# A cross-attention block on one core: steps taken in pairs, and the keys' jobs cut into halves and quarters

## The chip, the cores and the metric

The kernel runs on one core of a Trainium2 chip. The metric is the device time of one execution in microseconds (us). The five engines are named as in the profile: PE is TensorE (PEld its weight loads), DVE is VectorE, ACT is ScalarE, POOL is GpSimd and SP is SyncE, which issues most of the DMAs.

## What is computed

Three layers on x (4 batches x 256 tokens x 256 channels), each with a layernorm ahead and a residual: cross attention to a context of 4096 x 192 for each batch (16 heads of 16), windowed self attention, and a feed-forward with 16 banks of which each token takes two. The change is in the first layer:

```
q = layernorm(x) @ wq.T + bq          # 256 queries per batch
k = ctx @ wk.T + bk                   # 4096 keys per batch
v = ctx @ wv.T + bv
attn = softmax(q k.T / 4)             # per head, 256 x 4096
x = x + (attn v) @ wo.T + bo
```

## The kernel before

**Steps.** Four heads of a batch are a group; there are 16 groups. A group's 4096 keys are 32 tiles of 128, and one tile of a group is a step: 512 steps, numbered n. PE's program is written out by hand in the order of the steps (the loop at L886). A step of the main phase issues three things:

- `scores(n)` (L619, matmuls of L629): four matmuls, keys of tile n against 256 queries, into one of two pairs of PSUM banks. ACT takes the exponential from there into `wts` (L1162, one instruction of 128x1024).
- `max_pair(n + 36)` (L580, matmuls of L599): two matmuls of 512 columns for a group that comes later; DVE reduces each to its row maxima (`reduce_max`, L1412). These maxima are needed before a group's scores begin, hence the lead of 36 steps. From step 36 on the results rotate through three banks (`M_BANKS`), and the pair of number m waits until the first reduction of pair m-1 is done: `e.wait_ge(dve_max, maxed(2 * m - 2))` (L595).
- `weigh(n - 2)` (L634, matmuls of L647): the weights of step n-2 against the values, four heads side by side in four column strips of the array. In two steps of each group (t = 2 and 3) none and two of them are issued.

**Side jobs.** Between steps PE does jobs that `side_jobs(n)` (L133) puts at fixed steps: `("k", f)` projects 1024 keys (L513, 12 matmuls), `("v", b, j)` 256 values (L532), `neg`, `sum`, `norm` and `out` carry a group's maxima and its result. `n + LEAD + K_LEAD` is n + 52, so `("k", f)` stands behind step 16f - 52, and its keys are first read by `max_pair(16f)`, in step 16f - 36: 16 steps later. All jobs and scores share the two bank pairs in turn (`S_NO`), and `bank_pair(job)` (L493) lets PE start a job when ACT has emptied the job two before it.

**The way of a key job.** ACT copies it to `key_f` with the bias (L1169). POOL splits it into a high and a low part (`split_keys`, L1880: a cast, L1883, and a subtraction, L1885). SP copies both parts with twelve DMAs of 128 KB into `keys` (`scatter_k`, L2073; the DMAs are L2071). `max_pair(16f)` waits for all twelve: `e.wait_ge(ld_k[f % 4], k_landed(f))` (L588).

**Values.** In batches 1 to 3 a value job stands at every third step, 16 in a batch, over the first half of its preparation (steps 7, 10, 13, ... counted from where its window begins).

## Time and profile before

| | |
|---|---|
| timed runs (3) | 1278.29, 1279.77 (median), 1281.58 us |
| profiled execution, span from first to last instruction | 1276.3 us |
| median of the timed runs less that span | 3.5 us |
| PE busy | 1239.8 us, 97% of the span |
| DVE busy | 867.8 us, 68% |
| ACT busy | 718.2 us, 56% |
| POOL busy | 258.4 us, 20% |
| step 0 begins / the last scores begin | 74.6 / 917 us |

A matmul in fp32 is recorded as two matmuls of the profile (the weighings are four instructions and eight records). A busy PE is not PE at its peak: the end of a record is modelled, and records overlap. The steps are most of the kernel: some 842 us of the 1276.

### The profile page before, as it was taken

To read this page: it belongs to the slowest core of one execution; us is meant where nothing else is said; L and a number is where in the kernel's file an instruction comes from. 1 tells how busy PE (TensorE), PEld (TensorE's weight loads), DVE (VectorE), ACT (ScalarE), POOL (GpSimd) and SP (SyncE) were. 2 spreads that over 40 slices of the span, in tenths; PEclk is the share of its full clock that TensorE was granted. 3 is DMA by queue.
4 is the path that set the end of the run, shared out by engine and by line. 5 is a ranking of instruction groups with operands and counts; after the bars stand their busy time and mean duration, and the time that the engine had idled before them with its cause. 6 is when DMAs were issued, how large, how long until landed. Compare 5 with 4: busy or idle time off the path is not lost.

```text
span 1276.3 us, 29874 instructions
## 1 busy us (share of the span) xinstructions
PE 1239.8 (97%) x12312; PEld 710.2 (56%) x12312; DVE 867.8 (68%) x1663; ACT 718.2 (56%) x942; POOL 258.4 (20%) x258
## 2 busy tenths in 40 slices
PE   8999999999999999999999999999999998999998
PEld 5454444555544455544445554444466567777787
DVE  4988888766787967588886768894354686223234
ACT  4557777666677867676776767778433320112120
POOL 3322112211111211111211111202011243122210
PEclk9999999999999999999999999999999998999999
DMA  7833573533465554344663433321020005999993
GB/s 223 134 51 59 87 167 53 75 59 59 57 102 124 79 73 61 52 57 100 123 88 53 57 51 57 65 36 52 11 72 2 2 17 222 413 407 401 388 406 117
DMA packets 49847, 150.44 MB, mean 118 GB/s; under 512 B 16944, under 2 KB 23088, under 8 KB 41776
## 3 DMA queue, kind: packets, MB, share of 16 engines
q1 hardware_dynamic: 45552, 136.92, 45.4%
q0 software_dynamic: 2432, 7.11, 1.7%
q10 hardware_dynamic: 1728, 4.49, 1.0%
q8 instruction: 98, 1.61, 0.6%
q14 instruction: 37, 0.30, 0.1%
HBM read 90.03 MB, written 7.08 MB: 76 GB/s over the span
## 4 chain that ended last, share of the span: by engine, by line
PE 88%; DVE 5%; ACT 4%; issue 2%; POOL 1%; DMA 1%; ACTq 0%; DVEq 0%; POOLq 0%
PE psum L647 21%; PE psum L629 15%; PE psum L599 11%; PE psum L513 7%; PE psum L532 6%; PE psum L1072 5%; PE psum L1100 5%; ACT wts L1162 2%; PE psum L1097 2%; PE psum L1066 2%; PE psum L725 2%; DVE part_max L1402 1%; PE psum L845 1%; PE psum L719 1%; PE psum L675 1%
## 5 line engine op out<-in xcount | busy, mean ns | idle before, releaser
L1412 DVE TENSOR_REDUCE part_max<-psum 128x1 f32<-128x512 f32 x952 | 609.7, 685 | 164.0 <-PE psum L599 162.3
L1162 ACT ACTIVATE wts<-psum 128x1024 f32<-128x1024 f32 x512 | 515.8, 1023 | 93.8 <-PE psum L629 92.7
L647 PE MATMUL psum<-wts,vals 128*17 128x256 f32 x4096 | 317.3, 385 | 0.0
L629 PE MATMUL psum<-queries,keys 51*128 51x256 f32 x2048 | 260.6, 333 | 8.2 <-ACT wts L1162 7.0
L629 PEld LDWEIGHTS psum<-queries,keys 51*128 51x128 f32 x2048 | 157.5, 185 | 199.6 <-issue 141.6
L599 PE MATMUL psum<-keys,queries 51*128 51x512 f32 x1024 | 226.5, 438 | 8.7 <-ACT wts L1162 6.0
L647 PEld LDWEIGHTS psum<-wts,vals 128*17 128x17 f32 x4096 | 69.5, 95 | 120.4 <-issue 96.3
L1883 POOL CAST key_high<-key_low 128x1024 fp32r<-128x1024 f32 x31 | 32.2, 1038 | 394.4 <-ACT key_low L1169 390.1
L599 PEld LDWEIGHTS psum<-keys,queries 51*128 51x128 f32 x1024 | 96.7, 184 | 27.4 <-DVE part_max L1402 10.7
L532 PE MATMUL psum<-wv,ctx_in 64*128 64x256 f32 x768 | 100.1, 390 | 3.2 <-ACT key_low L1169 1.8
L1332 ACT ACTIVATE hid<-psum,b1s 128x128 f32<-128x128 f32 (+1 forms) x124 | 31.7, 351 | 113.5 <-PE psum L1072 77.1
L513 PE MATMUL psum<-ctx_in,wk 64*64 64x512 f32 x768 | 93.5, 599 | 0.0
L532 PEld LDWEIGHTS psum<-wv,ctx_in 64*128 64x128 f32 x768 | 70.0, 186 | 32.3 <-issue 17.6
L1169 ACT ACTIVATE key_low<-psum,bk 128x1024 f32<-128x1024 f32 x31 | 34.5, 1114 | 79.4 <-PE psum L513 79.4
L1175 ACT ACTIVATE vals<-psum 128x512 f32<-128x512 f32 x64 | 38.2, 598 | 67.2 <-PE psum L532 67.2
L1885 POOL TENSOR_TENSOR key_low<-key_low,key_high 128x1024 fp32r<-128x1024 f32 x31 | 73.7, 2377 | 2.6
L1921 POOL TENSOR_TENSOR o_norm<-o_raw,inverse 128x256 f32<-128x256 f32 x15 | 11.0, 736 | 268.7 <-ACT inverse L1196 268.7
L1072 PE MATMUL psum<-xTt,w1s 128*128 128x128 f32 x544 | 63.5, 275 | 0.0
L1072 PEld LDWEIGHTS psum<-xTt,w1s 128*128 128x128 f32 x544 | 62.2, 192 | 0.1
L1100 PE MATMUL psum<-w2s,hid 128*128 128x256 f32 x272 | 62.1, 382 | 0.0
L1812 DVE TENSOR_SCALAR hid<-psum,b1s 128x128 f32<-128x128 f32 (+1 forms) x124 | 30.5, 313 | 45.0 <-PE psum L1072 41.9
L1100 PEld LDWEIGHTS psum<-w2s,hid 128*128 128x128 f32 x272 | 50.4, 190 | 11.9 <-issue 5.7
(260 smaller groups left out, 1035.7 us busy)
## 6 DMA issues: line engine op xcount, KB each, us to landing
keys<-key_high SPq DMA_DIRECT2D x256, 128.0 KB, 4.3
w1s<-in_W SPq DMA_DIRECT2D x31, 1024.0 KB
w2s<-in_W SPq DMA_DIRECT2D x31, 1024.0 KB
keys<-key_low SPq DMA_DIRECT2D x128, 128.0 KB, 6.1
ctx_in<-in_ctxT SPq DMA_DIRECT2D x12, 768.0 KB, 8.5
ctx_in<-in_ctxT ACTq DMA_DIRECT2D x4, 768.0 KB, 12.4
rows_y<-in_zeros SPq DMA_DIRECT2D x1, 2048.0 KB, 8.6
queries<-query_high SPq DMA_DIRECT2D x60, 32.0 KB, 5.0
```

Of the source, the lines that this page charges most:

```text
L513: t = e.matmul(bank(S_BANKS[S_NO["k", f] % 2] + odd)[64 * i:64 * i + 64], wk[rows, g % NG, r * 64:(r + 1) * 64], ctx_in[rows, c // 2 + i, ...
L532: m = e.matmul(bank(first + odd)[:, 0:EMB], ctx_in[rows, p, at:at + P], wv[rows, r], start=(r == 0), stop=(r == CB - 1))
L599: e.matmul(bank(LEAD_BANKS[m % 2] + i if m < LEAD else M_BANKS[(2 * m + i) % 3]), queries[g % 3][64 * i:64 * i + STK, hh, qt * P:(qt + 1) ...
L629: m = e.matmul(bank(S_BANKS[S_NO["s", n] % 2] + i)[:, hh * SEQ:(hh + 1) * SEQ], keys[64 * i:64 * i + STK, hh, c, at:at + P], queries[g % 3 ...
L647: i = e.matmul(bank(O_BANK)[32 * j:32 * j + VW, 0:SEQ], vals[:, t, h * VW:(h + 1) * VW], wts[n % NW][:, j * SEQ:(j + 1) * SEQ], start=(t = ...
L1072: i = e.matmul(dst[:, q * P:(q + 1) * P], w1s[w[0]][:, k, hc * P:(hc + 1) * P], xTt[j % 2][:, k], start=(k == 0), stop=(k == KE - 1))
L1100: i = e.matmul(dst, hid[j % 2][:, hc], w2s[w[0]][:, hc], start=(hc == 0), stop=(hc == HC - 1))
L1162: i = e.activation(wts[n % NW], s_bank(job, 2), ACT.Exp, scale=QSCALE)
L1169: i = e.activation(key_f.rearrange("p c k -> p (c k)"), s_bank(job, 2), ACT.Identity, bias=bk[:, hg:hg + 1])
L1175: i = e.activation(vals[:, t:last + 1:CH // P].rearrange("p t (h w) -> p t h w", w=VW)[:, :, :, 0:HD], s_bank(job, 2).rearrange("p (t h w) ...
L1412: e.reduce_max(part_max[g % 2][:, hq, c:c + 1], bank(M_BANKS[n % 3]), AX_X).then_inc(dve_max, 1)
L1885: e.tensor_tensor(key_low, key_f, key_high.bitcast(F32), ALU.subtract).then_inc(split_low, 1)
```

## The change

**Steps in pairs.** PE's order for two steps n and n+1 (n even) is now: scores n, max pair n+36, scores n+1, weigh n-2, weigh n-1, max pair n+37, and then the side jobs of both steps. ACT takes both exponentials and then the side jobs. The lead phase (steps -36 to -1) is as before.

**Key jobs in parts.** `key_parts(f)` gives 1 part for f < 4, 2 parts for f >= 8 with f % 8 in (2, 3, 4), and 4 parts for all others. Parts stand behind steps 16f-52, 16f-50 (halves), and also 16f-48 and 16f-46 (quarters). POOL's split and SP's twelve DMAs come after the last part. K_LEAD, and with it the step in which the keys are first read, are not touched.

**Values.** The 16 value jobs of a batch stand at even steps 6, 8, 10, 16 to 26, 32 to 42 and 48 of the window.

```diff
@@ -130,17 +130,31 @@
         return self.sem
 
 
+def key_parts(f):
+
+    if f < 4:
+        return 1
+    return 2 if f >= 2 * NG and f % (2 * NG) in (2, 3, 4) else 4
+
+
+def key_jobs(f):
+
+    return [("k", f)] if key_parts(f) == 1 else [("k", f, q) for q in range(key_parts(f))]
+
+
+VALUES_AT = (6, 8, 10, 16, 18, 20, 22, 24, 26, 32, 34, 36, 38, 40, 42, 48)
+
+
 def side_jobs(n):
 
     jobs = []
     f, at = divmod(n + LEAD + K_LEAD, 4 * CH // P)
-    if at == 0 and 4 <= f < QUADS:
-        jobs.append(("k", f))
+    if 4 <= f < QUADS and at % 2 == 0 and at // 2 < key_parts(f):
+        jobs.append(key_jobs(f)[at // 2])
     jobs += FIRST_AT.get(n, [])
     b, at = divmod(n + KT, NG * KT)
-    j, off = divmod(at - 7, 3)
-    if 0 < b < BATCH and off == 0 and 0 <= j < KT // 2:
-        jobs.append(("v", b, j))
+    if 0 < b < BATCH and at in VALUES_AT:
+        jobs.append(("v", b, VALUES_AT.index(at)))
     g, at = divmod(n + KT, KT)
     if at == KT - 3 and 0 <= g < GROUPS:
         jobs.append(("neg", g))
```

```diff
@@ -157,24 +171,16 @@
 
 
 S_JOBS = [("k", 0)] + [("v", 0, _j) for _j in range(FIRST_V)] + [("k", 1)]
-for _n in range(-LEAD, STEPS):
-    S_JOBS += ([("s", _n)] if _n >= 0 else []) + side_jobs(_n)
+for _n in range(-LEAD, 0):
+    S_JOBS += side_jobs(_n)
+for _n in range(0, STEPS, 2):
+    S_JOBS += [("s", _n), ("s", _n + 1)] + side_jobs(_n) + side_jobs(_n + 1)
 S_NO = {job: n for n, job in enumerate(S_JOBS)}
 
 
 def maxed(n):
 
     return n // 2 + 1 if n < 2 * LEAD else n + 1 - LEAD
-
-
-def weighed_at(n):
-
-    t = n % KT
-    if n < 3 or (n < STEPS and t == 2):
-        return []
-    if n < STEPS and t == 3:
-        return [n - 3, n - 2]
-    return [n - 2]
 
 
 def v_tiles(j):
```

```diff
@@ -495,13 +501,16 @@
                 if S_NO[job] > 1:
                     e.wait_ge(act_s, S_NO[job] - 1)
 
-            def keys_of(f, part=None, pieces=range(CB)):
-
+            def keys_of(f, part=None, pieces=range(CB), job=None):
+
+                job = job or ("k", f)
                 g, c = f // 2, f % 2 * 4
+                width = CH // key_parts(f)
+                first = job[2] * width if len(job) > 2 else 0
                 pairs = range(2) if part is None else (part,)
                 if 0 in pieces:
                     if part is None:
-                        bank_pair(("k", f))
+                        bank_pair(job)
                     if f == 2:
                         e.wait_ge(ld_wk_rest, 16)
                     for i in pairs:
```

```diff
@@ -510,8 +519,9 @@
                     for i in pairs:
                         for odd in range(2):
                             rows = slice(64 * odd, 64 * odd + 64)
-                            t = e.matmul(bank(S_BANKS[S_NO["k", f] % 2] + odd)[64 * i:64 * i + 64],
-                                         wk[rows, g % NG, r * 64:(r + 1) * 64], ctx_in[rows, c // 2 + i, r * CH:(r + 1) * CH],
+                            at = r * CH + first
+                            t = e.matmul(bank(S_BANKS[S_NO[job] % 2] + odd)[64 * i:64 * i + 64, 0:width],
+                                         wk[rows, g % NG, r * 64:(r + 1) * 64], ctx_in[rows, c // 2 + i, at:at + width],
                                          start=(r == 0), stop=(r == CB - 1))
                 if CB - 1 in pieces:
                     t.then_inc(pe_first if part == 0 else pe_s, 1)
```

```diff
@@ -883,24 +893,33 @@
                 values_of(0, j)
             keys_of(1)
             done_early = 0
-            for n in range(-LEAD, STEPS + 2):
-                jobs = side_jobs(n) if n < STEPS else []
-                if 0 <= n < STEPS:
-                    scores(n)
+            for n in range(-LEAD, 0):
+                max_pair(n + LEAD)
+                for job, piece in LEAD_PIECES.get(n, ()):
+                    lead_piece(job, piece)
+                for job in side_jobs(n):
+                    if job not in LEAD_JOBS:
+                        side_job(job)
+            for n in range(0, STEPS, 2):
+                scores(n)
                 if n + LEAD < STEPS:
                     max_pair(n + LEAD)
-                for m in weighed_at(n):
-                    weigh(m)
-                for job, piece in LEAD_PIECES.get(n, ()):
-                    lead_piece(job, piece)
-                for job in jobs:
-                    if job not in LEAD_JOBS:
+                scores(n + 1)
+                if n:
+                    weigh(n - 2)
+                    weigh(n - 1)
+                if n + LEAD < STEPS:
+                    max_pair(n + 1 + LEAD)
+                for m in (n, n + 1):
+                    for job in side_jobs(m):
                         side_job(job)
-                if n >= LAST * KT + EARLY_FROM and n % 3 != 0 and done_early < 10:
-                    early(done_early)
-                    done_early += 1
-                if n in FIRST_MAX2:
-                    max2(0, FIRST_MAX2.index(n))
+                    if m >= LAST * KT + EARLY_FROM and m % 3 != 0 and done_early < 10:
+                        early(done_early)
+                        done_early += 1
+                    if m in FIRST_MAX2:
+                        max2(0, FIRST_MAX2.index(m))
+            weigh(STEPS - 2)
+            weigh(STEPS - 1)
             e.wait_ge(act_ocopy, GROUPS)
             e.matmul(bank(X_BANK)[:, 0:SEQ], lsel, o_raw, start=True, stop=True).then_inc(pe_lastnorm, 1)
```

```diff
@@ -1166,7 +1185,11 @@
                     if f == 1:
                         e.wait_ge(ld_first, 16 * 6)
                     e.wait_ge(ld_k[(f - 1) % 4], k_landed(f - 1))
-                    i = e.activation(key_f.rearrange("p c k -> p (c k)"), s_bank(job, 2), ACT.Identity, bias=bk[:, hg:hg + 1])
+                    width = CH // key_parts(f)
+                    first = job[2] * width if len(job) > 2 else 0
+                    i = e.activation(key_f[:, :, first:first + width],
+                                     s_bank(job, 2).rearrange("p (c k) -> p c k", c=2)[:, :, 0:width], ACT.Identity,
+                                     bias=bk[:, hg:hg + 1])
                 elif kind == "v":
                     b, j = job[1:]
                     t, last = v_tiles(j)
```

```diff
@@ -1234,15 +1257,18 @@
             for i in range(BT, TT):
                 e.activation(xn1[:, i], x[:, i], ACT.Identity, scale=rstd[:, i:i + 1], bias=sq[:, i:i + 1]).then_inc(act_rows1, 1)
             empty(("k", 1))
-            for n in range(-LEAD, STEPS):
-                if n >= 0:
-                    empty(("s", n))
-                if n > KT and n % KT == 1:
-                    ocopy(n // KT - 1)
+            for n in range(-LEAD, 0):
                 for job in side_jobs(n):
                     empty(job)
                 if n in ONES_AT:
                     key_ones(ONES_AT[n])
+            for n in range(0, STEPS, 2):
+                empty(("s", n))
+                empty(("s", n + 1))
+                if n and n % KT == 0:
+                    ocopy(n // KT - 1)
+                for job in side_jobs(n) + side_jobs(n + 1):
+                    empty(job)
             ocopy(LAST)
```

In POOL's and SP's programs and in the semaphore counts, `("k", f)` became the last part:

```diff
@@ -1878,7 +1904,7 @@
             own = Tally(pool_seq)
 
             def split_keys(f):
-                e.wait_ge(act_s, done(("k", f)))
+                e.wait_ge(act_s, done(key_jobs(f)[-1]))
                 e.wait_ge(ld_k[(f - 1) % 4], k_landed(f - 1))
                 e.tensor_copy(key_high, key_f).then_inc(split_high, 1)
                 e.wait_ge(split_high, f + 1)
```

```diff
@@ -2081,7 +2108,7 @@
                         scatter_pair(f, c, part, ld_k[f % 4])
 
             def load_ctx(b, p):
-                e.wait_ge(pe_s, done(("k", (NG * b - 1) * 2 + p // 2)))
+                e.wait_ge(pe_s, done(key_jobs((NG * b - 1) * 2 + p // 2)[-1]))
                 e.dma_start(ctx_in[:, p], a["ctxT"][b, p]).then_inc(ld_ctx[p], 16)
```

```diff
@@ -2104,7 +2131,7 @@
                     for dst, src in ((lsel, "lsel"), (wo, "woT"), (bv, "bv"), (bo_bc, "bo")):
                         e.dma_start(dst, a[src]).then_inc(ld_w, 16)
                 for job in side_jobs(n - 2):
-                    if job[0] == "k":
+                    if job[0] == "k" and job == key_jobs(job[1])[-1]:
                         scatter_k(job[1])
                         b, at = divmod(job[1], NG * 2)
                         if at >= (NG - 1) * 2 and b + 1 < BATCH:
```

**PE's order in plain steps.** PE, some steps in front of a key job; L629 are scores, L599 a max pair, L647 a weighing. The buffer of `wts` rises by one with each step. Before:

```order
L629 MATMUL psum<-queries_70,keys 128x256 x4
L599 MATMUL psum<-keys,queries_71 128x512 x2
L647 MATMUL psum<-wts_66,vals 17x256 x4
L629 MATMUL psum<-queries_70,keys 128x256 x4
L599 MATMUL psum<-keys,queries_71 128x512 x2
L647 MATMUL psum<-wts_67,vals 17x256 x4
```

And now (L639 scores, L609 max pair, L657 weighing):

```order
L639 MATMUL psum<-queries_70,keys 128x256 x4
L609 MATMUL psum<-keys,queries_71 128x512 x2
L639 MATMUL psum<-queries_70,keys 128x256 x4
L657 MATMUL psum<-wts_66,vals 17x256 x4
L657 MATMUL psum<-wts_67,vals 17x256 x4
L609 MATMUL psum<-keys,queries_71 128x512 x2
```

The two weighings stand together, and between the first and the second max pair there are now one scores and two weighings, between the second and the next first one scores alone.

**PE around a key job.** Before, the whole job (L513) stands behind one step:

```order
L647 MATMUL psum<-wts_68,vals 17x256 x4
L513 MATMUL psum<-ctx_in,wk 64x512 x12
L629 MATMUL psum<-queries_70,keys 128x256 x4
L599 MATMUL psum<-keys,queries_72 128x512 x2
L647 MATMUL psum<-wts_69,vals 17x256 x4
```

Now quarters (L523) stand behind the second max pair of pairs of steps; these are the last two of four, the second of them the part after which the split can begin:

```order
L609 MATMUL psum<-keys,queries_72 128x512 x2
L523 MATMUL psum<-ctx_in,wk 64x128 x12
L639 MATMUL psum<-queries_71,keys 128x256 x4
L609 MATMUL psum<-keys,queries_72 128x512 x2
L639 MATMUL psum<-queries_71,keys 128x256 x4
L657 MATMUL psum<-wts_66,vals 17x256 x4
L657 MATMUL psum<-wts_67,vals 17x256 x4
L609 MATMUL psum<-keys,queries_72 128x512 x2
L523 MATMUL psum<-ctx_in,wk 64x128 x12
```

From the last quarter to the max pair that reads these keys there are four pairs of steps and one scores, where 15 whole steps and one scores stood before.

**ACT.** Parts of a key job are emptied by copies of 128x2x128 (L1190) between two exponentials and the next two:

```order
L1190 ACTIVATE key_low<-psum,bk 128x2x128
L1181 ACTIVATE wts_68<-psum 128x1024
L1181 ACTIVATE wts_69<-psum 128x1024
L1190 ACTIVATE key_low<-psum,bk 128x2x128
L1181 ACTIVATE wts_66<-psum 128x1024
L1181 ACTIVATE wts_67<-psum 128x1024
```

Before, one exponential stood between jobs' copies wherever a step did.

## Rows read from the trace of the kernel before

**Rows 1.** The page: engines' shares of the span, and groups of instructions.

```profile
PE 1239.8 (97%) x12312; PEld 710.2 (56%) x12312; DVE 867.8 (68%) x1663; ACT 718.2 (56%) x942; POOL 258.4 (20%) x258
...
PE 88%; DVE 5%; ACT 4%; issue 2%; POOL 1%; DMA 1%; ACTq 0%; DVEq 0%; POOLq 0%
...
L1412 DVE TENSOR_REDUCE part_max<-psum 128x1 f32<-128x512 f32 x952 | 609.7, 685 | 164.0 <-PE psum L599 162.3
```

**Rows 2.** Timeline of PE, plain steps (start us, us, engine, line, operation).

```profile
403.02 0.50 PE L629 MATMUL psum<-queries,keys 51*128 51x256 f32 x4
403.36 0.45 PE L599 MATMUL psum<-keys,queries 51*128 51x512 f32 x2
403.74 0.63 PE L647 MATMUL psum<-wts,vals 128*17 128x256 f32 x8
404.29 0.50 PE L629 MATMUL psum<-queries,keys 51*128 51x256 f32 x4
```

**Rows 3.** Timeline of DVE over the same steps.

```profile
401.90 4.51 DVE L1412 TENSOR_REDUCE part_max<-psum 128x1 f32<-128x512 f32 x7
```

**Rows 4.** Timeline of PE, the two steps of a group with weighings together.

```profile
395.76 0.50 PE L629 MATMUL psum<-queries,keys 51*128 51x256 f32 x4
396.11 0.45 PE L599 MATMUL psum<-keys,queries 51*128 51x512 f32 x2
396.40 0.40 PE L629 MATMUL psum<-queries,keys 51*128 51x256 f32 x4
397.34 0.50 PE L599 MATMUL psum<-keys,queries 51*128 51x512 f32 x2 [0.55 <-ACT wts L1162]
397.77 1.06 PE L647 MATMUL psum<-wts,vals 128*17 128x256 f32 x16
398.76 0.50 PE L629 MATMUL psum<-queries,keys 51*128 51x256 f32 x4
```

**Rows 5.** Timeline of PE around a key job.

```profile
411.16 2.81 PE L513 MATMUL psum<-ctx_in,wk 64*64 64x512 f32 x24
413.90 0.50 PE L629 MATMUL psum<-queries,keys 51*128 51x256 f32 x4
414.24 0.39 PE L599 MATMUL psum<-keys,queries 51*128 51x512 f32 x2
414.56 0.63 PE L647 MATMUL psum<-wts,vals 128*17 128x256 f32 x8
```

**Rows 6.** Timelines of ACT, POOL and SP: the way of that job.

```profile
414.03 1.11 ACT L1169 ACTIVATE key_low<-psum,bk 128x1024 f32<-128x1024 f32 x1 [2.68 <-PE psum L513]
...
415.21 1.04 POOL L1883 CAST key_high<-key_low 128x1024 fp32r<-128x1024 f32 x1 [4.19 <-ACT key_low L1169]
...
421.39 2.50 SPq L2071 DMA_DIRECT2D keys<-key_low  x4
```

**Rows 7.** DMA issues in 423:424, the last two of its twelve copies.

```profile
keys<-key_low SPq DMA_DIRECT2D x2, 128.0 KB, 6.8
```

**Rows 8.** Timeline of PE: max pairs number 16f, f = 15 to 21.

```profile
410.17 0.50 PE L599 MATMUL psum<-keys,queries 51*128 51x512 f32 x2
...
433.43 0.49 PE L599 MATMUL psum<-keys,queries 51*128 51x512 f32 x2
...
461.88 0.50 PE L599 MATMUL psum<-keys,queries 51*128 51x512 f32 x2
...
491.40 0.50 PE L599 MATMUL psum<-keys,queries 51*128 51x512 f32 x2
...
523.25 0.40 PE L599 MATMUL psum<-keys,queries 51*128 51x512 f32 x2
...
553.73 0.50 PE L599 MATMUL psum<-keys,queries 51*128 51x512 f32 x2
...
579.12 0.50 PE L599 MATMUL psum<-keys,queries 51*128 51x512 f32 x2
```

**Rows 9.** Timelines of PE and ACT around a value job.

```profile
471.99 1.57 PE L532 MATMUL psum<-wv,ctx_in 64*128 64x256 f32 x12
473.20 0.59 PE L629 MATMUL psum<-queries,keys 51*128 51x256 f32 x4
473.63 0.40 PE L599 MATMUL psum<-keys,queries 51*128 51x512 f32 x2
...
473.60 0.60 ACT L1175 ACTIVATE vals<-psum 128x512 f32<-128x512 f32 x1 [1.33 <-PE psum L532]
```

**Rows 10.** Copies by ACT of other sizes, steps 0 to 511.

```profile
L1196 ACT ACTIVATE inverse<-psum 128x256 f32<-128x256 f32 x15 | 5.8, 385 | 3.1 <-PE psum L666 3.1
```

**Rows 11.** Windows in the last layer: us, busy times, granted clock, DMA.

```profile
1055.00:1065.00 10.00, 7.35 (x112) 6.58 (x109) 8.31 (x57) 1.08 (x4) 1.69 (x5) 1.00 0.13 49
1065.00:1068.50 3.50, 3.50 (x25) 2.00 (x26) 3.29 (x12) 0.00 (x0) 0.51 (x1) 0.51 0.35 56
```

More of the change, by code:

```diff
@@ L2106, in _ @@
                 for job in side_jobs(n - 2):
-                    if job[0] == "k":
+                    if job[0] == "k" and job == key_jobs(job[1])[-1]:
                         scatter_k(job[1])
```

5 lines of the change are left out of this document (3 added, 2 removed).

## Prediction

> **What bounds the kernel now.** The page comes first: PE is busy for 97% of the span and 88% of the chain that ended last is PE's, while DVE's reductions take 609.7 us and sat idle for 164 us before them, nearly all of it for PE's max pairs [rows 1]. That reads as PE bound, with DVE held up by PE's long side jobs. But a shares table is a mean over places with different limits, so PE's timeline comes next. A plain step takes 404.29 - 403.02 = 1.27 us (1.28 in most): 0.34 from scores to max pair, 0.38 from there to the weighing, 0.55 to 0.56 to the next scores [rows 2]. Over the same steps DVE ran seven reductions in 4.51 us without a gap, 0.64 each and 1.28 for two [rows 3]. Behind a key job, when DVE had caught up, the max pair's slot is 414.56 - 414.24 = 0.32 instead of 0.38 [rows 5]. So PE alone would need 0.34 + 0.32 + 0.56 = 1.22 us, and it waits some 0.06 in each plain step. What it waits for is the rule that a max pair follows the first reduction of the pair before it. This is a loop, matmul, first reduction, next matmul, and its length can be read where nothing else stands between two max pairs: 397.34 - 396.11 = 1.23 us [rows 4]; in plain steps it closes at 1.28. **PE's own work and the loop over the three banks are near each other, and the loop is what ends last in a plain step.**
>
> **Pairs of steps.** Two weighings in a row take 398.76 - 397.77 = 0.99 instead of 2 x 0.56, and a scores behind a max pair is not preceded by a change of the array's shape. Adding slots for PE alone: scores 0.34, max pair 0.22 (its 0.32 before a weighing less the 0.10 which a change seems to cost; half of what the weighings save is 0.07, so 0.07 to 0.10), scores 0.33, weighings 0.99, second max pair 0.33; the scores that follow then start loaded, 0.23 for 0.34. That is 2.10 us for two steps against 2.44 before. The Trainium skill (TensorEngine Tiling (Array Packing), Key Properties) says that changing the tiling mode drains the engine, where another tile of the same mode does not. The 0.99 agrees with it; by that rule alone every pair would gain 0.3 us, which is the first rival.
>
> The order of the max pairs speaks against it. From the first to the second there now lie a scores and two weighings: 0.29 + 0.33 + 0.99 = 1.61 us. From the second to the next first there is only one scores, so that distance is the loop's, 1.23 to 1.28. A pair of steps without a job thus takes 1.61 + 1.28 = 2.9 us, not 2.1 and not 2 x 1.28 = 2.56. The trace has the same instructions in nearly this order: the two steps where a group's weighings already stand together take 398.76 - 395.76 = 3.00 us, and their second max pair starts late [rows 4]. I take 2.9. In PE's 0.8 us of waiting a job can hide.
>
> **Parts of key jobs.** A whole job takes 413.90 - 411.16 = 2.74 us [rows 5]. Its columns are three rounds of twice 0.43, 2.56 in all, and 0.18 around them; these 0.18 are paid by each part. A quarter is 0.64 + 0.18 = 0.82 (bounds: 0.69, a quarter of the whole, and 1.21, a value job of as many matmuls [rows 9]); a half 1.46. ACT's copy of a quarter takes 0.39 to 0.60, between its copies of 256 and of 512 columns [rows 9, 10]; the second scores of the next pair now needs that copy's bank (the job two before it), and stands only 0.56 behind the first: 0.1 of waiting for a quarter, 0.3 to 0.4 for a half. Pair with a quarter: 0.34 + 0.22 + 0.33 + 0.99 + 0.43 (second max pair, loaded late and with a change of shape, as at 397.34 [rows 4]) + 0.82 + 0.1 = 3.25. With a half: 4.15.
>
> **When the keys land.** This is the largest term. For the job that ended at 413.9, ACT's copy ended at 415.1, POOL's cast at 416.25, SP issued twelve copies until 423.9 [rows 6], and the last two took 6.8 us to land [rows 7]: landed near 430, 16 us after the job's end. The max pair that reads them came at 433.43 [rows 8], so 3.4 us were to spare out of 19.5. Now the split starts behind the last quarter, six steps later, while the reader stays in its step. Less 0.7 for the shorter copy of ACT, the way is 15.4 us. Between them lie four pairs without a key job and one scores, 4 x 2.9 + 0.3 = 11.9 us. **PE waits about 3.5 us at each max pair 16f of a quartered job, with scores, weighings and both other engines queued behind it.** `sum` and `norm` hide in that time. Halves end two steps late and have value jobs behind them: six pairs, no wait.
>
> The stretch from one max pair 16f to the next is then:
> - f = 4, 6, 8, 14, 16, 22, 24, 30 (quarters, no group change): before 433.43 - 410.17 = 23.3; after 4 x 3.25 - 0.3 + 15.4 = 28.1. +4.8, eight times.
> - f = 5, 7, 13, 15, 21, 23, 29, 31 (quarters, with `neg`): before 25.4 (553.73 to 579.12); `neg` adds 0.9 as now: 29.0. +3.6, eight times.
> - f = 9, 17, 25 (quarters, three value jobs behind them): before 461.88 - 433.43 = 28.5; after 29.0. +0.5.
>
> Sum: 38 + 29 + 1.5 = 69 us.
>
> **Value jobs.** One adds 1.21 and slows the next scores by 0.09, 1.30. Its copy on ACT ends at 474.2, 1.0 behind the start of the scores after it [rows 9], where the second scores of a pair would start after 0.65: 0.35 to 0.45 lost. Pair: 0.43 + 0.6 + 0.44 + 0.99 + 0.33 + 1.1 = 3.9, against 1.21 + 2 x 1.28 = 3.77 for a value job and two steps now. f = 10, 18, 26 (two halves, six value jobs): 2 x 4.15 + 6 x 3.9 = 31.7 for 29.5; f = 11, 19, 27, with the group's jobs (1.9): 33.6 for 31.9; f = 12, 20, 28 (two halves, one value job, `out` at 5.9, four bare pairs): 8.3 + 3.9 + 5.9 + 11.6 = 29.7 for 30.5 [rows 8]. Sum: 3 x (2.2 + 1.7 - 0.8) = 9 us.
>
> **Ends.** Six pairs ahead of f = 4's first quarter, four of them with value jobs: +1. The eight pairs behind the last key job, 23.2 for 20.3: +3. From step 476 on there are no max pairs and ACT's 1.02 us exponential sets about 1 us a step in either order: 0. Everything behind the first layer is unchanged.
>
> **Forecast:** 69 + 9 + 4 = 82 us on the profiled execution's span of 1276.3 is 1358; the median of the runs lies 3.5 above that span, so **1361 us**.
>
> **Rivals.**
> 1. *Shape changes and idle DVE were the bound* (faster). If the loop over the banks closed sooner than I read it, and the keys landed in time, pairs without a job would go at DVE's pace when it is never kept waiting, 0.61 a reduction at best (an estimate from 0.64 less PE's wait of 0.06 for every second one), 2.44 us for 2.56; pairs with a job would gain 0.3. 128 x 0.1 + 110 x 0.3 = 46 us, less 10 for the parts' overheads: some 1244. For it stands the 97% of PE; against it the 3.00 us of [rows 4]. 6%.
> 2. *The pairs are slow, but the keys land in time.* The wait falls away if the way from the last part is under 12 us, as it would be if part of the twelve copies' time were only their queueing behind each other's issue. The stretches then take 13.0 - 0.3 + 11.9 = 24.6 (+1.3) and 25.5 (+0.1): 11 + 2 + 9 + 4 = 26 us, 1306. Against: the copies' issue alone takes 7.5 us of the 16 and does not change [rows 6]. 8%.
> 3. *The clock falls as well* (slower still). In 1055 to 1065 PE was busy for 7.35 of 10 us, and then its granted clock was 0.51, the lower of its levels (1.2 of 2.4 GHz), for 3.5 us [rows 11]. A wait of 3.5 us at each of 16 places may do the same; each such 3.5 us at half clock does 1.75 us of work less, 28 us: 1390. Against: PE is busy on both sides of the wait. The Trainium skill (TensorE: Matmul & The Clock Gate, The two states you'll see) has the clock fall to half after an idle window, so it speaks for this rival; no row here has a wait of that length. 8%.
> 4. The order of instructions, above, shows that the change does what it says; no chance is held for that.
>
> **How the numbers follow.** My forecast has the remaining 78%; its own range is 1320 to 1385, from the quarter's bounds (76 pairs, -0.15 to +0.2 each), the value pairs (52, -0.35 to +0.15) and the way of the keys (16, +-0.7). The range to hold 8 in 10 goes down to the second rival and up to the third: 1303 to 1392. A measurement of this kernel tells about 0.3%, 4 us, from no change. Faster: the first rival, 6%. Same: 2%, a mild case of the second. Slower: 92%.
>
> **What would show it.** In the changed profile: max pairs 16f of quartered jobs with 3 to 4 us of idle PE before them, ended by a DMA on `keys`; stretches of 28 to 29 us where 23.3 and 25.4 stood; pairs without a job at 2.9; weighings of two steps in one block of 0.99; PE's busy share down to 90% or less; DVE's idle before L1412 up by some 80 us. It is wrong if pairs without a job take under 2.6 us, if the keys' wait is under 1 us, or if the value pairs and not the key stretches carry the loss.

## The result and the profile after

The changed kernel takes 1416.9 us (median of 4 runs, 1410.87 to 1431.14) where the kernel before, on the same chip, takes 1280.67 (1278.29 to 1282.1): 1.108 times as long, with an interval of 1.1022 to 1.1138. The forecast was 1361, with a range of 1303 to 1392. Its direction and most of its mechanisms hold; the loss is 136 us where it said 82. (The profiled execution has a span of 1417.6 us, 141 more than before's 1276.3; the sums below go by the spans.)

The page after (busy time and share of the span, instructions; the chain's shares; then groups with idle time ahead of them), against [rows 1]:

```profile
PE 1276.5 (90%) x13896; PEld 794.4 (56%) x13896; DVE 873.0 (62%) x1663; ACT 721.4 (51%) x1008; POOL 257.6 (18%) x258
...
PE 68%; SPq 8%; DMA 8%; ACT 6%; DVE 5%; issue 2%; POOL 2%; ACTq 0%; POOLq 0%; DVEq 0%
...
L1438 DVE TENSOR_REDUCE part_max<-psum 128x1 f32<-128x512 f32 x952 | 612.9, 686 | 301.7 <-PE psum L609 300.9
...
L609 PE MATMUL psum<-keys,queries 51*128 51x512 f32 x1024 | 251.9, 489 | 93.8 <-DMA keys<-key_low 56.8
```

The work is nearly the same (PE 1276.5 us for 1239.8, DVE 873.0 for 867.8), and the span has grown by 141. SP's queue and the copies of the keys, which were nowhere in the chain, now hold 16% of it. DVE waits 138 us longer for its max pairs. The waits after (in total, times, longest):

```profile
PEld psum L609 <- DVE part_max L1438: 148.7, 280, 1.2
...
PE psum L609 <- DMA keys<-key_low: 56.8, 16, 4.2
...
PEld psum L639 <- ACT vals L1198: 26.8, 52, 0.6
```

Sixteen max pairs wait for their keys, 3.55 us in the mean: the forecast's 3.5 us. PE's timeline shows pairs of steps without a job and then such a wait, where [rows 2] had plain steps:

```profile
432.11 0.50 PE L609 MATMUL psum<-keys,queries 51*128 51x512 f32 x2
432.45 0.40 PE L639 MATMUL psum<-queries,keys 51*128 51x256 f32 x4
433.39 0.50 PE L609 MATMUL psum<-keys,queries 51*128 51x512 f32 x2 [0.55 <-DVE part_max L1438]
433.73 0.40 PE L639 MATMUL psum<-queries,keys 51*128 51x256 f32 x4
434.05 1.06 PE L657 MATMUL psum<-wts,vals 128*17 128x256 f32 x16
435.04 0.50 PE L609 MATMUL psum<-keys,queries 51*128 51x512 f32 x2
...
439.57 0.50 PE L609 MATMUL psum<-keys,queries 51*128 51x512 f32 x2 [3.80 <-DMA keys<-key_low]
...
471.25 0.64 PE L609 MATMUL psum<-keys,queries 51*128 51x512 f32 x2 [3.76 <-DMA keys<-key_low]
...
500.95 0.50 PE L609 MATMUL psum<-keys,queries 51*128 51x512 f32 x2 [3.70 <-DMA keys<-key_low]
```

From max pair to max pair it is 433.39 - 432.11 = 1.28 us with one scores between them, and 435.04 - 433.39 = 1.65 with a scores and the double weighing: 2.93 for a pair of steps. The rows at 439.57, 471.25 and 500.95 are max pairs 16f for f = 14, 15 and 16: stretches of 31.7 and 29.7 us, where [rows 8] have 25.4 and 23.3.

The windows (us, busy time of PE, PEld, DVE, ACT, POOL, granted clock, DMA share, GB/s) behind two of the waits, and over the last steps:

```profile
437.00:440.70 3.70, 1.13 (x18) 0.75 (x22) 1.34 (x6) 0.35 (x1) 0.00 (x0) 1.00 1.00 249
440.70:444.10 3.40, 3.40 (x44) 1.80 (x38) 2.05 (x4) 0.78 (x2) 0.00 (x0) 0.50 0.58 233
...
973.20:1010.80 37.60, 35.10 (x248) 17.66 (x246) 21.44 (x37) 17.30 (x17) 0.00 (x0) 0.50 0.00 1
```

Behind the wait that ended at 439.57 the granted clock is 0.50 for 3.4 us: the lower level, 1.2 of 2.4 GHz. The same is found at each of the 16 waits, for 3.4 to 10.2 us, and behind the last one, at 972.6, it stays at 0.50 for 37.6 us. In all, 112 us of the steps run at the lower level (in this sense "the clock is low" below), 106 of them at the 16 waits. The Trainium skill (TensorE: Matmul & The Clock Gate, HAM oscillation) describes a kernel in which each wait for a DMA sends the clock down; the trace agrees.

The stretches from max pair 16(f - 1) to max pair 16f, in us (where several stand together, their mean), with two of the experiments below:

| f | before | forecast | after | e5_fill | e3_early |
|---|---|---|---|---|---|
| 6, 8, 14, 16, 22, 24, 30 | 23.3 | 28.1 | 30.1 | 28.3 | 25.2 |
| 5, 7, 13, 15, 21, 23, 29, 31 (`neg`) | 25.4 | 29.0 | 31.3 | 30.2 | 27.8 |
| 9, 17, 25 (`neg`) | 28.5 | 29.0 | 31.3 | 33.0 | 32.8 |
| 10, 18, 26 | 29.5 | 31.7 | 31.5 | 31.5 | 32.2 |
| 11, 19, 27 | 31.8 | 33.6 | 34.6 | 34.6 | 34.7 |
| 12, 20, 28 | 30.5 | 29.7 | 30.3 | 30.3 | 28.4 |

In sum, the 141 us of span are 9.9 ahead of max pair 64, 117.3 from there to max pair 496 (844.1 for 726.8), 12.1 from there to the last scores (83.7 for 71.6), and 2 elsewhere.

### The profile page after: what moved, and what is told of

Same layout as the page of the kernel before. It is cut to its first block, busy times and chain, and to the rows that moved or that the text cites. A ratio compares the mean times of both kernels' runs of the same rounds, so it can differ in the third digit from the quotient of the medians.

```text
span 1417.6 us, 33240 instructions
## 1 busy us (share of the span) xinstructions
PE 1276.5 (90%) x13896; PEld 794.4 (56%) x13896; DVE 873.0 (62%) x1663; ACT 721.4 (51%) x1008; POOL 257.6 (18%) x258
## 4 chain that ended last, share of the span: by engine, by line
PE 68%; SPq 8%; DMA 8%; ACT 6%; DVE 5%; issue 2%; POOL 2%; ACTq 0%; POOLq 0%; DVEq 0%
PE psum L657 14%; PE psum L609 9%; PE psum L639 8%; SPq L2098 8%; PE psum L523 8%; DMA keys<-key_low 7%; PE psum L542 5%; PE psum L1091 4%; PE psum L1119 4%; ACT vals L1198 2%; PE psum L1116 2%; PE psum L1085 2%; ACT key_low L1190 2%; PE psum L735 2%; DVE part_max L1438 1%
## 5 line engine op out<-in xcount | busy, mean ns | idle before, releaser
L1181 ACT ACTIVATE wts<-psum 128x1024 f32<-128x1024 f32 x512 | 504.5, 1023 | 146.6 <-PE psum L639 146.0
L609 PE MATMUL psum<-keys,queries 51*128 51x512 f32 x1024 | 251.9, 489 | 93.8 <-DMA keys<-key_low 56.8
L657 PE MATMUL psum<-wts,vals 128*17 128x256 f32 x4096 | 290.1, 403 | 0.0
L639 PE MATMUL psum<-queries,keys 51*128 51x256 f32 x2048 | 247.7, 323 | 25.5 <-ACT vals L1198 10.2
L639 PEld LDWEIGHTS psum<-queries,keys 51*128 51x128 f32 x2048 | 176.8, 193 | 108.5 <-ACT key_low L1190 29.5
L609 PEld LDWEIGHTS psum<-keys,queries 51*128 51x128 f32 x1024 | 100.0, 192 | 235.7 <-DVE part_max L1438 148.7
L657 PEld LDWEIGHTS psum<-wts,vals 128*17 128x17 f32 x4096 | 96.7, 99 | 93.1 <-issue 14.4
L1190 ACT ACTIVATE key_low<-psum,bk 128x256 f32<-128x256 f32 (+2 forms) x97 | 51.8, 534 | 134.6 <-PE psum L523 134.6
L523 PE MATMUL psum<-ctx_in,wk 64*64 64x128 f32 (+2 forms) x2352 | 115.7, 324 | 0.0
L542 PE MATMUL psum<-wv,ctx_in 64*128 64x256 f32 x768 | 96.2, 380 | 3.2 <-ACT key_low L1190 1.8
L523 PEld LDWEIGHTS psum<-ctx_in,wk 64*64 64x64 f32 x2352 | 72.2, 141 | 36.2 <-issue 17.9
L1358 ACT ACTIVATE hid<-psum,b1s 128x128 f32<-128x128 f32 (+1 forms) x124 | 31.7, 351 | 113.6 <-PE psum L1091 77.3
L1838 DVE TENSOR_SCALAR hid<-psum,b1s 128x128 f32<-128x128 f32 (+1 forms) x124 | 30.5, 314 | 45.0 <-PE psum L1091 41.8
```

The source lines that it names most:

```text
L523: t = e.matmul(bank(S_BANKS[S_NO[job] % 2] + odd)[64 * i:64 * i + 64, 0:width], wk[rows, g % NG, r * 64:(r + 1) * 64], ctx_in[rows, c // 2 ...
L542: m = e.matmul(bank(first + odd)[:, 0:EMB], ctx_in[rows, p, at:at + P], wv[rows, r], start=(r == 0), stop=(r == CB - 1))
L609: e.matmul(bank(LEAD_BANKS[m % 2] + i if m < LEAD else M_BANKS[(2 * m + i) % 3]), queries[g % 3][64 * i:64 * i + STK, hh, qt * P:(qt + 1) ...
L639: m = e.matmul(bank(S_BANKS[S_NO["s", n] % 2] + i)[:, hh * SEQ:(hh + 1) * SEQ], keys[64 * i:64 * i + STK, hh, c, at:at + P], queries[g % 3 ...
L657: i = e.matmul(bank(O_BANK)[32 * j:32 * j + VW, 0:SEQ], vals[:, t, h * VW:(h + 1) * VW], wts[n % NW][:, j * SEQ:(j + 1) * SEQ], start=(t = ...
L1181: i = e.activation(wts[n % NW], s_bank(job, 2), ACT.Exp, scale=QSCALE)
```

## Experiments

Each ran beside the kernel before, which took 1280 us each time. Ratios carry 95% intervals; lines of code are those of each kernel.

### Which part of the change costs what

**e1_whole: the pairs, with key jobs in one piece.**

```diff
 def key_parts(f):
-    if f < 4:
-        return 1
-    return 2 if f >= 2 * NG and f % (2 * NG) in (2, 3, 4) else 4
+    return 1
```

> Steps in pairs as in the change, but every key job whole again (one part, 16 steps ahead of its reader). Theory 'late keys' (the last part comes six steps later while its reader stays, so PE waits about 4 us at 16 places, and its clock falls behind that wait): the waits are gone, PE's granted clock stays at 1.0 through the steps, stretches without a group change go from 29.7 to about 26 to 27 us (seven pairs of 2.93, one of 5.7 that holds a whole job and the wait for its copy), about 1345. Rival 'pairing' (the order of the max pairs makes the loss by itself): within 25 us of the change, above 1390. Rival 'parts' (the overhead of 12 matmuls and a copy for each part): like the first in time, but without idle PE before max pairs 16f in the change's own trace, which that trace speaks against.

Measured: 1374.99 us, 1.0712 (1.0663 to 1.0761). The key waits are gone and 94 us are left, 30 more than I took the late keys to leave. Its timeline of PE at a whole job shows what I had not counted:

```profile
425.66 2.81 PE L521 MATMUL psum<-ctx_in,wk 64*64 64x512 f32 x24
428.40 0.40 PE L623 MATMUL psum<-identb,neg_parts 128*3 128x128 bf16 x8
429.70 0.51 PE L637 MATMUL psum<-queries,keys 51*128 51x256 f32 x4 [0.91 <-ACT key_low L1188]
...
430.92 0.50 PE L637 MATMUL psum<-queries,keys 51*128 51x256 f32 x4 [0.48 <-ACT queries L1209]
```

Both scores of the next pair wait for ACT: the first for the key job's copy (0.91), the second for `neg`'s (0.48), since the banks are emptied in turn. A pair with a whole job takes 5.18 us and one with `neg` as well 7.89, and the clock is low for 48 us of the steps. So this run undoes the late keys but puts something else in their place; it does not price them.

**e2_parts: the steps and values of before, with the change's parts.** `key_parts`, `key_jobs` and the copies by part are the change's, everything else is before's.

```diff
-    if at == 0 and 4 <= f < QUADS:
-        jobs.append(("k", f))
+    if 4 <= f < QUADS and at % 2 == 0 and at // 2 < key_parts(f):
+        jobs.append(key_jobs(f)[at // 2])
```

> The steps and value jobs as before the change, key jobs in halves and quarters as in the change. Theory 'late keys': with 1.28 us a step the last quarter again comes about 12 us ahead of its reader, so the waits of 3 to 4 us are there without any pairing, the clock falls behind them, and a stretch without a group change takes 15.4 + 12.1 + 1.5 = 29 us for 23.3: about 1375. Rival 'pairing': within 25 us of the kernel before, under 1306, with little wait at max pairs 16f.

Measured: 1365.77 us, 1.0668 (1.0636 to 1.07). Its waits:

```profile
PE psum L618 <- DMA keys<-key_low: 45.3, 16, 3.8
```

The parts alone cost 85 us, with no steps in pairs: 45.3 us of waits, and a low clock for 102 us. (1375 was expected.)

**e3_early: the change, with all key jobs four steps earlier.**

```diff
-LEAD, K_LEAD = 36, 16
+LEAD, K_LEAD = 36, 20
```

> The change with one number set otherwise: key jobs start 20 steps ahead of the step in which they are read less 36, not 16 (K_LEAD = 20), so the last quarter stands 14 steps ahead of its reader, six pairs of 2.93 = 17.6 us against a way of 15.4. Theory 'late keys': no wait on the copies at any max pair 16f, no fall of the clock in the steps, stretches without a group change 4 x 3.33 + 4 x 2.93 = 25.0 us for 29.7; 16 x 4.6 = 74 us and some clock at the ends: about 1335. A small wait (under 1 us) may move to ACT, whose copy of the next job's first quarter waits for the same landing. Rival 'pairing': less than 25 us is gained, above 1390.

Measured: 1342.53 us, 1.0483 (1.0453 to 1.0514). No max pair waits for a DMA, the clock is low for 7 us of the steps, and 74 of the 136 us come back. Pairs without a job still take 2.93. A new line stands in its waits:

```profile
ACT key_low L1190 <- DMA keys<-key_low: 22.4, 13, 2.2
```

**e8_parts_early: e2, with all key jobs four steps earlier.**

```diff
-LEAD, K_LEAD = 36, 16
+LEAD, K_LEAD = 36, 20
```

> The steps and values as before the change, key jobs in parts, started four steps earlier (K_LEAD = 20), so the reader stands 14 steps behind the last quarter. Theory 'one buffer for the keys': ACT may copy a job's first quarter only when the job before has landed (the same buffer), so a stretch cannot be under the way, 15.4 us, and the time from the first to the last quarter, 6 steps and 3 quarters or 10.1 us: 25.5 us for 23.3, whatever the lead, with the wait now ahead of ACT's first copy. About +2 us at 16 stretches, 1 at 9: about 1320. Rival 'the reader's place was all': stretches of 24.0 us (only the overhead of parts, 0.5 to 0.8), under 1300.

Measured: 1311.97 us, 1.025 (1.023 to 1.0269). Late keys cost 54 us in the old order of steps (1365.8 less 1312.0) and 74 in pairs. What is left are 32 us, with the same wait as in e3:

```profile
ACT key_low L1190 <- DMA keys<-key_low: 32.1, 15, 3.0
```

ACT copies into one buffer, `key_f`, which is free only when the job before has landed in `keys` (the wait on `ld_k` at the head of the copy). So the first part of job f+1 comes behind the landing of job f, and its own landing comes later by the spread of the parts and the way of 15.4 us. With quarters a stretch without a change of group takes 24.0 to 25.4 us, 24.8 in the mean, where before's is 23.3 and 25.5 were expected. Not all of the 32 us are the buffer's: the parts have their own overhead, and in the stretches f = 11, 19 and 27 the run meets what e9, next, shows at large (33.9 us, where e13 below has 32.4).

**e9_halves_early: e8 with all jobs in halves.** The parts are spread over two steps, not six.

```diff
     if f < 4:
         return 1
-    return 2 if f >= 2 * NG and f % (2 * NG) in (2, 3, 4) else 4
+    return 2
```

> As e8_parts_early (steps and values as before the change, keys started four steps earlier), every job in two halves instead of four quarters. Theory 'one buffer for the keys': the way and two steps with a half, 15.5 + 2 x 1.28 + 1.5 = 19.6 us, are under the stretch, so no wait ahead of ACT's copy, and only the second part's overhead is left, some 0.5 us at 28 jobs: about 1293, stretches 23.8. Rival 'each part costs some 1 us wherever it stands': 28 x 1 = 28, about 1308, near e8_parts_early.

Measured: 1358.47 us, 1.0609 (1.0553 to 1.0664), a miss by 65 us. The stretches without a group's change are 23.3, as the theory of the one buffer says, and ACT waits for no DMA. But of the eight with `neg` that took 25.4, six take 29.6 to 33.2, one 40.2 and the last 27.5. There DVE's small cast, 0.18 us before, takes 1.98. The POOL, DVE and PE rows:

```profile
410.52 2.36 POOL L1908 TENSOR_TENSOR key_low<-key_low,key_high 128x1024 fp32r<-128x1024 f32 x1
...
410.93 1.98 DVE L1443 CAST neg_parts<-neg_max 128x8 bf16<-128x8 f32 x1
...
414.32 0.80 PE L618 MATMUL psum<-keys,queries 51*128 51x512 f32 x2 [2.70 <-DVE part_max L1435]
```

The cast ends at 412.91, POOL's subtraction at 412.88. The reductions queue behind the cast, PE waits 2.70 us for one of them, and then its clock is low: 89 us of the steps. The new lead had put POOL's subtraction beside the cast in 13 of 15 groups. In one more group the cast began 0.02 us ahead of POOL and took its 0.18, and the operation behind it, DVE's subtraction of two operands, was held instead, until 177.71 where POOL's ends at 177.69:

```profile
175.33 2.36 POOL L1908 TENSOR_TENSOR key_low<-key_low,key_high 128x1024 fp32r<-128x1024 f32 x1
...
175.31 0.18 DVE L1443 CAST neg_parts<-neg_max 128x8 bf16<-128x8 f32 x1
175.52 2.19 DVE L1445 TENSOR_TENSOR neg_rest<-neg_max,neg_parts 128x8 f32<-128x8 f32 x1
```

e8 has the long cast in three groups (f = 11, 19, 27); the change itself has none.

**e13_halves_18: e9 with K_LEAD = 18**, which moves the subtraction two steps away and leaves the last half where the whole job was before.

```diff
-LEAD, K_LEAD = 36, 20
+LEAD, K_LEAD = 36, 18
```

> As e9_halves_early, with key jobs started two steps later (K_LEAD = 18): the last half stands where the whole job stood before the change, and GpSimd's split no longer runs over DVE's small casts at a group's end, which took 1.98 us instead of 0.18 in e9_halves_early at 13 of 15 groups. Theory 'the casts waited for GpSimd': casts 0.18, stretches of a group's end back from 29.6 to 33 to about 26, the clock at 1.0, about 1288. Rival 'halves are dear at a group's end wherever GpSimd runs': again above 1330.

Measured: 1284.29 us, 1.0039 (1.0026 to 1.0051), 74 us less than e9 for two steps of lead. All casts but the first take 0.18 us (178 to 181 ns; the first 477, before 478), the stretches 23.3 and 25.6, as the theory has it. So halves as such cost 5 us, and gain nothing.

### The loop over the banks

**e4_order: e3, with both scores ahead of the first max pair.**

```diff
                 scores(n)
+                scores(n + 1)
                 if n + LEAD < STEPS:
                     max_pair(n + LEAD)
-                scores(n + 1)
```

> As e3_early, and in a pair of steps both scores stand ahead of the first max pair: scores, scores, max, weigh, weigh, max. Theory 'loop over the banks': from the first to the second max pair only the two weighings are left (0.33 + 0.99 = 1.32), from the second to the next first two scores (0.9, so the loop's 1.28): a pair without a job takes 2.6 us instead of 2.93. Against it stands the second scores, which now comes 0.3 us earlier behind a job and so waits longer for ACT's copy: pairs with a value job 4.0 to 4.1 us for 3.92. About 110 bare pairs x 0.33 = 36 us less, some 10 given back: about 1310. Rival 'PE's own work bounds the pair': the same time as e3_early within 5 us.

Measured: 1364.22 us, 1.064 (1.0608 to 1.0671): 22 slower than e3, and a miss. The loop does what was expected of it, a pair without a job falls from 2.93 to 2.69. But the second scores now comes right behind the first and needs the bank of the side job. Its timeline of PE:

```profile
393.30 0.89 PE L523 MATMUL psum<-ctx_in,wk 64*64 64x128 f32 x24
394.12 0.50 PE L639 MATMUL psum<-queries,keys 51*128 51x256 f32 x4
395.55 0.50 PE L639 MATMUL psum<-queries,keys 51*128 51x256 f32 x4 [0.93 <-ACT key_low L1190]
```

A pair with a quarter takes 3.61 for 3.33. And where a pair without a job is quicker, ACT only comes sooner to the one buffer `key_f` and waits there: 36.6 us in all, 15 times, instead of the 22.4 of e3. The clock is low for 31 us of the steps, for 7 in e3, and this too is in the loss.

### The clock's share

**e5_fill: the change, with small matmuls in place of PE's idle time.** Ahead of the keys' wait, 54 matmuls of 128 columns go to the bank that the max pair will overwrite.

```diff
                     f = m // 16
+                    if f >= 4 and key_parts(f) == 4:
+                        e.wait_ge(dve_max, maxed(2 * m - 2))
+                        for _ in range(54):
+                            e.matmul(bank(M_BANKS[2 * m % 3])[:, 0:P], identb, identb, start=True, stop=True)
                     e.wait_ge(ld_k[f % 4], k_landed(f))
```

> The change, with 54 small matmuls (128 columns, bf16, some 3.0 us in all) on PE between the freed bank and the wait for the copies, at each max pair 16f of a job in quarters; their results are overwritten. They take up PE's waiting of about 4 us and change nothing else. Theory 'the clock fell behind the waits': the waits on the copies are as long in sum, PE's granted clock stays at 1.0 or nearly so in the steps (112 us at the lower level in the change), stretches without a group change go from 29.7 to about 28.2, those with one from 31.5 to about 29.5, the last 48 steps from 76 to 68 us: about 1377. Rival 'the clock costs nothing here, since the bank loop and the copies set the pace': within 8 us of the change, above 1409.

Measured: 1391.49 us, 1.0873 (1.0849 to 1.0898). It does 3.2 us more work at each of 19 places, 16 of them those of the waits, and is 25 us faster than the change; 1377 was expected, 14 less. Its timeline of PE, and its windows around this place:

```profile
431.36 3.19 PE L601 MATMUL psum<-identb 128*128 128x128 bf16 x54 [0.55 <-DVE part_max L1442]
434.65 0.50 PE L613 MATMUL psum<-keys,queries 51*128 51x512 f32 x2
```

```profile
427.00:433.00 6.00, 4.90 (x69) 3.47 (x65) 5.04 (x12) 3.37 (x4) 0.00 (x0) 1.00 1.03 133
433.00:441.00 8.00, 7.14 (x112) 4.50 (x109) 3.92 (x7) 4.28 (x6) 0.95 (x2) 1.00 0.58 198
```

The clock stays at 1.00 here, and is low for 7 us of the steps instead of 112. The stretches without `neg` fall from 30.1 to 28.3, and the end from 83.7 to 72.1, near before's 71.6. At f = 9, 17 and 25 the keys had landed 3.3 to 3.5 us before the max pair: there the change waits for next to nothing, and the fill costs its whole 3.2 us. On the spans, the clock's price in the change is therefore 1417.6 - 1390.1 + 3 x 3.2 = 37 us. The change's own four runs point the same way: between those of 1409.1 and 1429.3 us of span the mean granted clock goes from 0.965 to 0.945, which is some 59 us more at the lower level for 20 us of time; at that rate 112 us cost some 39 (an estimate).

### A better version

The pairs do save shape changes, and lose the gain to unequal distances between max pairs. So from here on the order of before stays, and only the weighing is held back for one step, where a side job makes the step long anyway.

**e6_values** holds it back in steps with a value job, **e7_both** in those with a key job as well, **e10_all** in those with any job.

The main lines of the edit in e7 (e6 has `("v",)` for `("v", "k")`, and e10 only `side_jobs(n)`):

```diff
-    if n < 3 or (n < STEPS and t == 2):
-        return []
...
+    for n in range(2, STEPS + 2):
+        due.append(n - 2)
+        t = n % KT
+        late = n < 3 or t == 2 or (len(due) < 2 and t not in (1, 3) and any(job[0] in ("v", "k") for job in side_jobs(n)))
+        if n >= STEPS or not late:
+            out[n], due = due, []
```

> The kernel before with one rule: in a step with a value job the weighing is left to the next step, so PE's order is scores, max, values, scores, max, weigh, weigh. The value job then stands among matmuls of its own shape, the two weighings together, and the two max pairs are 1.7 us apart on either side, above the loop's 1.28. Theory (two changes of shape saved, about 0.12 each, and weights loaded ahead; nothing else in the way): a value job and two steps take 3.4 us for 3.77, 52 of them: about 17 us less, 1263. Rival 'the bank loop or ACT's copy takes the gain back, as in the change': within 5 us of before.

> As e6_values, and the same rule in steps with a key job. Keys have a shape of their own, so one change of shape is saved, 0.12 to 0.2 us at each of 28 jobs: 3 to 5 us less than e6_values, about 1259. Rival: no difference from e6_values, if DVE, which has caught up behind a key job, is what the steps after it wait for.

> As e7_both, the weighing left to the next step in every step with a side job of any kind. Theory: sum, norm, neg and out use the full array, so again one change of shape is saved, 0.1 us at some 45 jobs: 3 to 5 us less than e7_both, 1256. Rival: the bank loop or ACT's copies set the pace around these small jobs: within 2 us of e7_both.

Measured: 1267.91 us for e6, 0.9906 (0.9891 to 0.9921); 1260.7 for e7, 0.9855 (0.9839 to 0.9872); 1266.57 for e10, 0.9895 (0.9879 to 0.9912). The timeline of PE of e7 at a key job:

```profile
542.94 0.49 PE L609 MATMUL psum<-keys,queries 51*128 51x512 f32 x2
543.37 2.81 PE L523 MATMUL psum<-ctx_in,wk 64*64 64x512 f32 x24
546.10 0.50 PE L639 MATMUL psum<-queries,keys 51*128 51x256 f32 x4
546.44 0.40 PE L609 MATMUL psum<-keys,queries 51*128 51x512 f32 x2
546.77 1.06 PE L657 MATMUL psum<-wts,vals 128*17 128x256 f32 x16
```

The long step and the one behind it take 5.29 us together for 5.39, two steps with a value job between them 3.48 for 3.77. e10's expectation failed: it is 6 us slower than e7. Its stretches f = 11, 19 and 27 take 31.9 where e7 has 30.2, and those with `neg` 25.4 for 24.8, while f = 12, 20 and 28 gain 0.7. Holding a weighing back behind the group's short jobs gives more back than it gains; by which wait was not followed further.

**e11_wait: e7, with a wait for each matmul of a max pair. e12_wait_alone: the same on the kernel before.** The pair waited as a whole until the first reduction of the pair before was done, but its first matmul only needs the bank that the reduction ahead of it has freed.

```diff
-                    e.wait_ge(dve_max, maxed(2 * m - 2))
+                    e.wait_ge(dve_max, maxed(2 * m - 3))
...
                 for i in range(2):
+                    if i and m > LEAD:
+                        e.wait_ge(dve_max, maxed(2 * m - 2))
```

> As e7_both, and each of the two matmuls of a max pair waits for its own bank alone: the first for the second reduction two pairs back, the second, as both do now, for the first reduction of the pair before. Theory 'loop over the banks': the loop of 1.28 us is broken, since the first matmul no longer waits for that reduction; a plain step falls to what PE and DVE each need, 1.22 us; some 290 plain steps x 0.05 = 14 us less than e7_both: about 1247. Rival 'the two matmuls then no longer run side by side': PE loses up to 0.2 us a pair, 1300 and more; or, if PE's order of issue is what sets 1.28, no difference.

> The kernel before with the split wait of e11_wait alone. Theory 'loop over the banks': plain steps 1.22 for 1.277, some 330 of them: 15 to 19 us less than before, about 1263. Rivals as in e11_wait: no difference, or 1300 and more.

Measured: 1252.09 us for e11, 0.9781 (0.9765 to 0.9797), the fastest of all; 1270.74 for e12, 0.9923 (0.9907 to 0.9939). e11's timelines of PE and DVE, against [rows 2] and [rows 3]:

```profile
380.91 0.51 PE L641 MATMUL psum<-queries,keys 51*128 51x256 f32 x4
381.25 0.45 PE L611 MATMUL psum<-keys,queries 51*128 51x512 f32 x2
381.63 0.63 PE L659 MATMUL psum<-wts,vals 128*17 128x256 f32 x8
382.19 0.51 PE L641 MATMUL psum<-queries,keys 51*128 51x256 f32 x4
...
383.41 0.51 PE L641 MATMUL psum<-queries,keys 51*128 51x256 f32 x4
```

```profile
380.46 3.78 DVE L1424 TENSOR_REDUCE part_max<-psum 128x1 f32<-128x512 f32 x6 [0.93 <-PE psum L611]
```

Scores to scores is 1.28 and 1.22 us in turn, where it was 1.28 each time. DVE takes 0.63 a reduction for 0.64. e12 alone gave 10 us where I had written 17, and e11 9 less than e7 where I had written 14: only every second step falls to 1.22, so half of the 0.06 us is gained. The loop over the banks was near PE's own work, as the prediction had it, and little was left to gain.

## Why the prediction was wrong in size

**What held.** *Pairs without a job*: 2.93 us, forecast 2.9, set by the bank loop (e4 shortens it by moving one scores). The 1.23 us that the prediction took for the loop has ACT as its releaser in [rows 4]; the rows after, at 433.39, name DVE's reduction, and the loop is 1.28. *Quarter pairs*: 3.33, forecast 3.25 (its terms add up to 3.23). *The quarter itself*: 394.12 - 393.30 = 0.82, as forecast; its upper bound, a value job "of as many matmuls", was misread, since a value job has six of 256 columns (12 records, [rows 9]) and a quarter twelve of 128 (24 records). *Value pairs*: 3.92, forecast 3.9. *The way of the keys*: 14.9 to 16.3 us from the last part's end at the 16 waits, forecast 15.4. *The keys' waits*: 3.55 us in the mean at 16 places, forecast 3.5. With the clock held up, in e5, the stretches without a group's change are 28.2 to 28.8, forecast 28.1. The first two rivals (pairs that gain, keys in time) are out.

**What failed.** On the span the forecast was +82 and the result +141. The 59 us between them are:

- *The clock, 37 us.* The prediction made it a rival, rival 3, with 28 us and 8%, instead of putting it in the sum. e5's span is 27.5 us under the change's, and 3 x 3.2 us of it are fill that covers no wait. 26 of the 37 lie in the stretches, close to the rival's 28; the rest is the end (83.7 less 72.1), with the 37.6 us at the lower level behind the last wait, which no row of before let me expect. The step that failed is the one that kept the clock out of the sum and gave it 8%, and the reason given for it, that PE is busy on both sides of the wait. In [rows 11] the clock had already fallen with PE busy for 7.35 of 10 us, and here PE was busy for 1.13 of 3.7. With the rival's 28 us in the sum the forecast would have been 1390, still 27 short.
- *`neg`, 12 us.* The step "`neg` adds 0.9 as now: 29.0" was short: with the clock at 1.00, in e5, the eight odd stretches take 30.2, and f = 9, 17, 25 would take 33.0 - 3.2 = 29.8. The timelines of PE and ACT there:

```profile
438.21 0.50 PE L643 MATMUL psum<-queries,keys 51*128 51x256 f32 x4 [0.27 <-ACT key_low L1194]
438.55 0.39 PE L613 MATMUL psum<-keys,queries 51*128 51x512 f32 x2
439.43 0.50 PE L643 MATMUL psum<-queries,keys 51*128 51x256 f32 x4 [0.48 <-ACT queries L1215]
...
440.84 0.50 PE L613 MATMUL psum<-keys,queries 51*128 51x512 f32 x2
```

```profile
437.69 0.47 ACT L1194 ACTIVATE key_low<-psum,bk 128x256 f32<-128x256 f32 x1 [1.24 <-PE psum L523]
438.18 1.19 ACT L1215 ACTIVATE queries<-psum 3x512 fp32r<-3x512 f32 x2
```

  A quarter and `neg` stand in one pair, so each of the next two scores waits for a copy, 0.27 and 0.48, and the max pairs are 440.84 - 438.55 = 2.29 apart instead of 1.65. Before, a step with its own work lay between the two scores. I had applied this rule of the banks to the quarter's copy and the value's, and not to `neg`'s. That is 0.64 us in each of 11 stretches, 7 of the 12 us. In f = 13, 21 and 29 another 0.7 us each is DVE's: it makes the group's negated maxima just there, five small operations from 376.26 to 377.38, and the second max pair of the stretch waits for the reduction behind them:

```profile
378.17 0.49 PE L613 MATMUL psum<-keys,queries 51*128 51x512 f32 x2 [0.67 <-DVE part_max L1442]
```

  What is left, 2 to 3 us, are ways of the keys that took up to 16.4 us, and fill that ran a little longer than the wait.
- *Value jobs and ends.* The stretches f = 10 to 12 and their like are 4 us over: value pairs with `sum` or `norm` take 4.97 us for the 3.92 of others, by the same rule. The quartered stretches without `neg` are 28.3 for 28.1, 2 us. Ahead of max pair 64 it is 9.9 for 5.8, 4 us. The end, without the clock, is 72.1 for before's 71.6 where 3 us more were forecast, so 2.5 us less: the eight pairs cost their 3 us (22.2 for 19.2 in e5), but the steps without max pairs, which the prediction put at no difference, take 49.9 for 52.4. 2 us lie outside the steps.

**How the parts share the loss.** Two ways through the runs give it. In pairs: keys that land late, with the lower clock behind them, cost 1416.9 - 1342.5 = 74 us; the rest, 62, is e3. In the old order: late keys 1365.8 - 1312.0 = 54, quarters with keys in time 1312.0 - 1279.9 = 32 (ACT's wait for the single buffer, the parts' own overhead, and some 4 us of the long casts), and then pairs on top of that 1342.5 - 1312.0 = 31. The terms are not additive to the microsecond, since each kernel waits for something else, and e1, pairs with whole jobs, is 94 us over by other waits; but each is a loss by itself. For "pairs, with keys in time" the second rival had +26, and e3 shows +62: the single buffer `key_f` and the banks behind `neg`, `sum` and `norm` were missing from it. How much of the difference each of them makes was not taken apart.

**What stays open.** No run tells why the clock stayed down at the end and came back behind the other waits. How much of the value pairs' waiting a different set of steps would save was not tried.

## What to carry to other kernels

When the last piece of a producer's work moves later, its whole way to the consumer moves with it: add the way up from the trace (here copy, split, twelve copies, landing, 15.4 us) and compare it with the steps that are left, and check the buffers at its head as well as the wait at its end. When an order is grouped, look at the distances between equal instructions and not at their sum; a loop over a few banks pays for the longest distance and gets nothing back for the short one. A new wait of several us on TensorE (3.0 to 4.2 us here) should be priced with the lower clock behind it, in the sum and not beside it.

## What the hardware showed beyond that

- DVE's cast of 128x8 took 1.98 us instead of 0.18 when POOL's two-input operation over 128x1024 ran, and ended with it (412.91 and 412.88); where the cast was first by 0.02 us, DVE's next operation, of two operands, took 2.19 us and ended with POOL's. The Trainium skill (SBUF — State Buffer, Who interferes with whom) says that casts on DVE may take a pair of ports that is shared with POOL, and that the loser waits for the whole instruction; e9 and e13 agree, with 1.98 and 0.18 us.
- From 973.2 on the granted clock stayed at 0.50 for 37.6 us although PE was busy for 35.1 of them; behind the wait at 439.57 it was back at 1.00 after 3.4 us, and at the 15 waits ahead of the last never later than after 10.2 us.
- 3.2 us of matmuls whose results nobody reads made a kernel 25 us faster, since they kept the clock at 1.00 through the waits for the keys.
